# Dense attention of a transformer layer: the softmax bias moved from a VectorE add to a one-row matmul into the scores' PSUM bank

## What is computed

```python
qkv = einsum('bsd,ed->bse', x, qkv_w) + qkv_b      # 16 heads of 64
scores = einsum('bhqe,bhke->bhqk', q, k) / 8
attn = softmax(scores, axis=-1)                    # over 2048 keys
out = einsum('bhqk,bhke->bhqe', attn, v)
out = einsum('bsd,ed->bse', out, proj_w) + proj_b
```

## Time and profile before

| | us |
|---|---|
| median of 3 runs (slowest core) | 4963.6 |
| lowest, highest | 4956.99, 5117.1 |
| the profiled execution | 4957.78 |
| its span, first to last instruction, slowest core (5) | 4956.2 |
| spans of the eight cores | 4939.3 to 4956.2 |
| busy: TensorE, VectorE, ScalarE, GpSimd | 3283.3, 1895.8, 1262.4, 198.1 |

### The profile page before, as it was taken

How to read it: one execution, slowest core, us unless ns; L and a number is a source line. 1 busy time by engine, 2 the same in 40 slices (tenths; PEclk the granted TensorE clock), 3 DMA queues, 4 the chain that set the end, 5 groups by cost and what they waited for, 6 DMA issues and landing times. The chain is left out here.

```text
span 4956.2 us, 40555 instructions; the slowest of 8 cores (4939.3 to 4956.2 us)
## 1 busy us (share of the span) xinstructions
PE 3283.3 (66%) x11024; PEld 1115.4 (23%) x11024; DVE 1895.8 (38%) x2135; ACT 1262.4 (25%) x1431; POOL 198.1 (4%) x204
## 2 busy tenths in 40 slices
PE   2655774774774764266776879697667768696971
PEld 0212111111111111022222234243212212242430
DVE  2121772772772773533223231322332232313225
ACT  2212551551551552011211311110112112211111
POOL 0000001001001000000000001010000000010100
PEclk8777776786776786666565689799656665897985
DMA  4002003003003005100000036464000000363653
GB/s 105 1 0 22 1 1 34 1 1 34 1 1 33 2 1 106 26 0 1 0 0 1 9 47 74 63 77 64 0 1 1 0 1 1 47 73 39 77 64 119
DMA packets 268624, 139.44 MB, mean 28 GB/s; under 512 B 161760, under 2 KB 252000, under 8 KB 266368
## 3 DMA queue, kind: packets, MB, share of 16 engines
q0 software_dynamic: 255024, 98.88, 17.3%
q1 hardware_dynamic: 13392, 37.97, 2.4%
HBM read 218.80 MB, written 16.78 MB: 48 GB/s over the span
## 5 line engine op out<-in xcount | busy, mean ns | idle before, releaser
L643 DVE TENSOR_TENSOR tmp<-psD,sqbuf 128x1024 f32<-128x1024 f32 x512 | 627.2, 1225 | 138.6 <-PE psD L633 83.2
L652 ACT ACTIVATE PTbuf<-tmp 128x1024 bf16<-128x1024 f32 x512 | 541.0, 1057 | 387.1 <-DVE tmp L643 355.2
L1094 ACT ACTIVATE PTA<-psA,s_cf 128x1024 bf16<-128x1024 f32 x224 | 249.5, 1114 | 1097.2 <-PE psA L1082 1068.2
L633 PE MATMUL psD<-qTO,kT 64*128 64x512 bf16 x1024 | 352.6, 478 | 191.6 <-DVE tmp L643 106.7
L668 PE MATMUL psD<-PTbuf,vTM 128*65 128x512 bf16 x1024 | 349.7, 443 | 65.0 <-ACT PTbuf L652 48.8
L1251 PE MATMUL psF<-xhat,w1b 128*128 128x512 bf16 x1408 | 338.7, 384 | 63.5 <-DVE xhat L1225 59.6
L1257 PE MATMUL psF<-xhat,w1b 128*128 128x512 bf16 x1408 | 332.8, 379 | 0.0
L1267 DVE SCALAR_TENSOR_TENSOR Gbuf<-psF,s_b1i,gel 128x512 bf16<-128x512 f32 x176 | 132.2, 751 | 499.0 <-ACT gel L1264 499.0
L1292 PE MATMUL psF<-Gbuf,w2b 128*128 128x512 bf16 x1408 | 310.0, 383 | 13.1 <-DMA w2b<-w2p 7.4
L1068 PE MATMUL psA<-qv,kb 64*128 64x512 bf16 x448 | 254.9, 569 | 8.8 <-DVE x_res L1175 6.1
L1114 DVE CAST lsumsA<-psA 1x512 bf16<-1x512 f32 x32 | 21.9, 685 | 588.6 <-PE psA L1108 588.6
(11 more groups left out here) (201 smaller groups left out, 3149.4 us busy)
## 6 DMA issues: line engine op xcount, KB each, us to landing
w1b<-w1i POOLq DMA_DIRECT2D x88, 512.0 KB, 6.0
w2b<-w2p POOLq DMA_DIRECT2D x32, 704.0 KB, 7.8
x_res<-xT SPq DMA_DIRECT2D x1, 8192.0 KB, 29.0
wQ<-wqT POOLq DMA_DIRECT2D x32, 256.0 KB, 4.5
wP<-projT POOLq DMA_DIRECT2D x32, 256.0 KB, 4.5
xsave<-x_res SPq DMA_DIRECT2D x1, 8192.0 KB, 41.6
xo<-xsave SPq DMA_DIRECT2D x4, 2048.0 KB, 14.0
yT<-tmpo SPq DMA_DIRECT2D x4, 2048.0 KB
```

The source lines that it names most:

```text
L633: tsm[par_h] = ph.op("tensor", lambda e, kc=kc, r0=64 * par_h, bank=bank, c=c: e.matmul(pb[:, bank, :], kT[r0:r0 + 64, c, kc * 128:kc * 12 ...
L643: v_addg[(kg, par_h, c)] = ph.op("vector", lambda e, par_h=par_h, bslot=bslot: e.tensor_tensor(tmp2[:, par_h * 2:par_h * 2 + 2, :], pb[:, ...
L652: s_expg[(kg, par_h, c)] = ph.op("scalar", lambda e, par_h=par_h, ptbase=ptbase: e.activation(pt[:, ptbase:ptbase + 2, :], tmp2[:, par_h * ...
L1094: s_expg[(kg, par_h, c)] = ph.op("scalar", lambda e, par_h=par_h, ptbase=ptbase: e.activation(pt[:, ptbase:ptbase + 2, :], pb[:, par_h * 2 ...
```

## The change

The bias is no longer spread over the partitions and added by VectorE. Each QK matmul leaves its accumulation open (`stop=False`), and a second matmul into the same bank, with the one-row stationary operand `c_on[0:1, 0:128]` (ones) and the head's bias row as moving operand, adds it there. ScalarE's exp reads PSUM directly. QK of the next group now waits for the exp that reads its banks, not for an add. Since the moving operand has to lie in partition 0, eight rows of `bq16` are laid side by side into `bneg1` by a DMA on SP at the start of a block, and the other eight by a second one after the QK of pair 3's last group; pair 0 and pair 4 wait for them. `tmp2`, `bnegb`, the selector matmuls and the copies are gone, and with them the wait of the first square of the norm for the last add.

```diff
-        bnegb = b.sq
-        tmp2 = sb2("tmp2", [128, 4, QB], F32)
+        bneg1 = sb2("bneg1", [1, 8, QB], BF16)
...
+            l_bn = ph.dma("sync", bneg1[0:1, :, :], bq16[0:8, :].unsqueeze(1),
+                          waits=[("V", v_bq)], sem="Lx")
...
-                for par_h in range(2):
-                    h = 2 * c + par_h
-                    bslot = (c % 2) * 2 + par_h
-                    wts = [("V", v_bq)]
-                    if v_addg.get((7, par_h, c - 1)) is not None:
-                        wts.append(("V", v_addg[(7, par_h, c - 1)]))
-                    t_s = ph.op("tensor", lambda e, h=h, par_h=par_h: e.matmul(
-                        pb[:, par_h * 2, :], b.c_selh[:, h * 128:h * 128 + 128],
-                        bq16[:], start=True, stop=True), waits=wts, inc="T")
-                    v_bb[bslot] = ph.op("vector", lambda e, bslot=bslot, par_h=par_h: e.tensor_copy(
-                        bnegb[:, bslot, :], pb[:, par_h * 2, :]), waits=[("T", t_s)], inc="V")
...
-                                prev_add = v_addg.get((kg - 1, par_h, c)) or v_addg.get((7, par_h, c - 1))
-                                if kg == 0:
-                                    waits.append(("V", v_bb[(c % 2) * 2 + par_h]))
-                                if prev_add is not None:
-                                    waits.append(("V", prev_add))
-                                tsm[par_h] = ph.op("tensor", lambda e, kc=kc, r0=64 * par_h, bank=bank, c=c: e.matmul(
+                                if c == 0 and kg == 0 and par_h == 0 and j2 == 0:
+                                    waits.append(("Lx", l_bn))
+                                if c == 4 and kg == 0 and par_h == 0 and j2 == 0:
+                                    waits.append(("Lx", l_bn1))
+                                prev_exp = s_expg.get((kg - 1, par_h, c)) or s_expg.get((7, par_h, c - 1))
+                                if prev_exp is not None:
+                                    waits.append(("S", prev_exp))
+                                ph.op("tensor", lambda e, kc=kc, r0=64 * par_h, bank=bank, c=c: e.matmul(
                                     pb[:, bank, :], kT[r0:r0 + 64, c, kc * 128:kc * 128 + 128],
-                                    qto[r0:r0 + 64, c, :], start=True, stop=True,
-                                    tile_position=(r0, 0)), waits=waits, inc="T")
+                                    qto[r0:r0 + 64, c, :], start=True, stop=False,
+                                    tile_position=(r0, 0)), waits=waits)
+                                tsm[(par_h, j2)] = ph.op("tensor", lambda e, bank=bank, h=h: e.matmul(
+                                    pb[:, bank, :], b.c_on[0:1, 0:128],
+                                    bneg1[0:1, h % 8, :], start=False, stop=True), inc="T")
+                        if c == 3 and kg == 7:
+                            l_bn1 = ph.dma("sync", bneg1[0:1, :, :],
+                                           bq16[8:16, :].unsqueeze(1),
+                                           waits=[("T", tsm[(1, 1)])], sem="Lx")
...
-                            v_addg[(kg, par_h, c)] = ph.op("vector", lambda e, par_h=par_h, bslot=bslot: e.tensor_tensor(
-                                tmp2[:, par_h * 2:par_h * 2 + 2, :],
-                                pb[:, par_h * 2:par_h * 2 + 2, :],
-                                bnegb[:, bslot:bslot + 1, :].broadcast_to([128, 2, QB]),
-                                ALU.add), waits=aw, inc="V")
                             ptbase = (kg % 2) * 4 + par_h * 2
-                            wts = [("V", v_addg[(kg, par_h, c)])]
+                            wts = [("T", tsm[(par_h, 0)]), ("T", tsm[(par_h, 1)])]
...
-                                pt[:, ptbase:ptbase + 2, :], tmp2[:, par_h * 2:par_h * 2 + 2, :],
+                                pt[:, ptbase:ptbase + 2, :], pb[:, par_h * 2:par_h * 2 + 2, :],
```

More of the change, by code:

```diff
@@ L597, in phase_dense @@
                 inc="V")
+            l_bn = ph.dma("sync", bneg1[0:1, :, :], bq16[0:8, :].unsqueeze(1),
+                          waits=[("V", v_bq)], sem="Lx")
+            l_bn1 = None
             v_oev = None
@@ L600, in phase_dense @@
             s_expg = {}
-            v_addg = {}
-            v_bb = {}
             t_av = {i: 0 for i in range(8)}
@@ L621, in phase_dense @@
                         for par_h in range(2):
+                            h = 2 * c + par_h
                             for j2 in range(2):
@@ L746, in phase_dense @@
                     sqw2 = [("S", s_att[0]), ("S", s_att[1])]
[L747 to L750, removed]
                 s_sq1 = ph.op("scalar", lambda e, c=c: e.activation(
```

## The result

The changed kernel takes 5615.0 us (median of 10 runs, 5551.5 to 5675.6) beside 5028.3 us of the kernel before in the same comparison (4957.0 to 5117.1): ratio **1.12**, 95% interval 1.111 to 1.129, slower. In some runs of either kernel one half of the chip shows a lower clock; they pull both medians up and are left out of the ratio (the lowest runs are 5551.5 and 5553.8 against 4957.0 and 4963.6). The profiled execution took 5551.5 us against 4957.8, so 593.7 us more; the forecast had 575 us more, but as an absolute time 5535 in a range of 5400 to 5610, and the median is 5 us above the upper end of that range.

What follows compares the result with a forecast made beforehand. VectorE's add was taken to bound D2 before, TensorE after. Eight pairs of 47.5 us plus 2.5 and 0.3 make a block 382.8 against 239.0; four add 575 to 4957.8: 5533, stated as 5535, range 5400 to 5610 us.

Steps and rivals of the forecast that it cites:

- The step: D2's pair loop on TensorE: each change in the number of contracted rows costs 0.11 us, QK to one-row included.
- The clock: TensorE in D2's blocks: granted clock 0.50 to 0.58, high 4% of the time, as in the local attention's sequence.
- Rivals A and B: D2's TensorE clock: A, high without gaps, 4909 us, 4%; B, stays near 0.80, 5095 us, 9%.
- A pair: Eight groups of D2 on TensorE: 48.9 us at the low clock, 28.0 at the high, 47.5 taken.
- The ends: D2's block ends: first QK 0.3 us later, second DMA hidden, last copy 2.5 us behind the last AV.
- The exp: ScalarE's exp in D2, reading PSUM directly: 1.11 us, as L1094 takes 1114 ns.
- The sum: D2's blocks: 382.8 us against 239.0 each, four blocks +575 us, 5533 us, stated as 5535.
- Rivals C and D: D2's one-row matmul: C, runs beside QK, 4985 us, 2%; D, QK to one-row step free, 5423 us, 12%.
- The step that failed: Whole kernel, profiled execution to median: median of the runs shown 6 us above the profiled one, so 5535 us.
- The range: Whole kernel: 5400 to 5610 us, with under 2 in 10 outside.
- E: D2's step costs 0.14 us in both directions, 61 us more, 5595, or an unseen wait, above 5610; 7%.
- The likeliest case: Whole kernel, the forecast's own case alone: 5490 to 5580 us for a clock share of 1% to 8%.

Runs made afterwards that it cites:

- e3: Changed kernel with the one-row matmuls ordered QK, QK, bias, bias for each head instead of QK, bias, QK, bias: 5468.8 us.
- e2: Changed kernel with the bias matmul contracting 64 rows at its QK's place in the array: 4809.0 us, ratio 0.976 to the kernel before.
- e1: Changed kernel with the bias matmul contracting 128 rows instead of one, all but one zero: 4942 us.
- e7: Changed kernel, one-row bias, with AV of two groups in one go after every second group, so eight AV in a row: 5425.6 us.
- e5: e2's 64-row bias with banks dealt by key tile, both heads' matmuls side by side, one exp for both heads: 4687.4 us.
- e4: Changed kernel without any bias matmul, the exp using another scale and a constant bias, so another softmax: 4731.4 us.
- e8: e5 with the bias matmul contracting one row again, in partition 0 for head 0 and 64 for head 1: 5033.0 us.

## Why the prediction was right and where it was wrong

- **The step.** Forecast 0.11 us at each change, also at QK to one-row, which no row showed. Right: 0.53 to 0.54 between starts, and e3 took 32 of them out of a pair for 3.5 us. The Trainium skill's rule (TensorEngine Tiling (Array Packing), Key Properties), that a change of mode drains the engine while a change of tile does not, agrees with both: the changes in the number of rows cost 0.11 us, and e2's two heads, 64 rows each on different halves of the array, start 13 ns apart.
- **The clock.** Forecast 0.50 to 0.58, 4% of the time high; measured 0.52, which is 4%. The reason given (the local attention's sequence) was right and e1 and e7 show it: here it is the instruction of few rows that holds the clock down, and the eight AV that bring the spells. The 4% was half of the local attention's 8% by eye, and that it fits is in part luck: with four times the runs of eight AV, e7 was high for 19 to 24% of its blocks and not for 16. Rivals A and B fell: TensorE is busy for 383 of 386 us at 0.52, while e5 is busy for 138 of 166 us and has 0.97. The Trainium skill's advice to keep TensorE busy (TensorE: Matmul & The Clock Gate, Why this matters for your kernels) was not enough here.
- **A pair.** Forecast 48.9 us at the low clock and 47.5 on the mean; measured 49.0 without a spell, 46.9 with one, 47.9 on the mean of block 0's first seven (502.19 to 837.14). A spell saves 2.1 us, less than the 2.5 in the sum (3.4 x 0.75), because it falls on QK and bias with their steps (1.07 us a pair of them against 0.64), not on AV, and TensorE is idle for 0.1 of its 3.4 us.
- **The ends.** First QK 2.2 us after `bq16` is ready (forecast 2.0); the second DMA hidden, as only the four waits at the block starts show (14.4 us in all, 3.6 each). The last copy ends 2.4 us behind the last AV (forecast 2.5).
- **The exp.** Forecast 1.11 us from PSUM, taken from L1094; measured 1.02. L1094 has a bias operand and this exp has none (e4, with one, has 1114 ns). It changed nothing, since ScalarE waits for TensorE.
- **The sum.** A block 386.4 us against 382.8, four blocks about 588 of the 594 us (the other three last 384.3, 386.5 and 386.5); of the remaining 6 us, 5.7 lie between the blocks, where the projection and the next queries are worked out (401.4 us against 395.7), and the stages behind D2 kept their length (3102.6 against 3101.4). Forecast 575, 3% too little: the 13 us in the blocks come from the pair's mean, 48.0 us over the first seven pairs of the four blocks against 47.5.
- **Rivals C and D** fell: one row never ran beside QK in this order, though it does beside the other head's one-row matmul in e8, and no step was free.
- **The step that failed** is the last one, from the profiled execution to the median: "The median of the runs shown is 6 us above the profiled one; I say 5535". That term came from three runs, which already went to 5117.1. Over ten runs the median lies 63.5 us above the profiled execution for the changed kernel (5615.0 to 5551.5) and 70.6 us for the kernel before (5028.3 to 4957.8). The sentence adds only 2 of its 6 us (5533 + 6 is 5539). Of the 80 us between 5535 and 5615, this term accounts for 61 and the sum above for 19. As ratios, 5533/4957.8 = 1.116 was forecast and 1.12 measured: the mechanism held, and the offset was mis-sized.
- **The range** had no room for it: both ends, 5400 and 5610, were bounded by the costs of instructions alone, and the upper end should have had the spread of the runs on top of E. The likeliest case was also stated too wide: a clock share of 1% gives a pair of 48.5 us and 5567 us, not 5580, which is the share of 0%.

## What to carry to other kernels

In this kernel a matmul that contracts one row cost its full 512 columns (0.427 us at the low clock), a step of 0.11 us on either side, and the clock of everything around it. If a rank-one term has to go into PSUM, give it the rows and the array place of its neighbours, even if all but one of them are zero: the same arithmetic went from 5551 to 4809 us. And with contractions of 64 rows put the matmuls of the two halves of the array next to each other in program order, with buffers cut so that one exp frees both: 4687 us, where VectorE's add had 4957. When forecasting an absolute time, take the distance from the profiled execution to the median, and its spread, from more than three runs.

## What was not expected of the hardware

- Granted clock in D2's blocks with the same columns and the same order, by the rows of the bias matmul: 0.52 with 1 and with 32, 0.92 to 0.94 with 64 (without steps), 0.95 to 0.98 with 128 (with steps).
- TensorE starts a matmul on the other half of the rows 13 ns after the first although three others of the first head stand between in the program (e2, 565.24). The four QK in 1.04 us in the earlier trace rows are such an overlap too, with one other between: at the low clock, 0.50 there, four in a row would take 1.7 us.
- The exp from PSUM without a bias operand takes 1023 ns, with one 1114 (e4, L1094) for 128 x 1024; the prediction took the second for the first.
